# Graph network kernel: the row sums that give edges their places move from ScalarE to VectorE

## The reference

```python
# layer 0: sums of the edges' attributes by the edge's source
aggr_msg = jax.ops.segment_sum(edge_attr, row, num_segments=x.shape[0])   # row = src
h = jnp.concatenate([x, aggr_msg], axis=-1)                               # x normalised, relu
h = jax.nn.relu(h @ W1 + b1)
out = h @ W2 + b2
# layer 1: attention over the edges of a destination
z = h @ W_fc.T
a = z_src @ blk[0] + z_dst @ blk[K] + ex @ w_e      # and terms of moments
att = jnp.where(a > 0, a, SLOPE * a)
m = jax.ops.segment_max(att, dst, num_segments=N)
expv = jnp.exp(att - m[dst])
w = expv / denom[dst]
msg = w[:, None] * (z_src + ez)
return jax.ops.segment_sum(msg, dst, num_segments=N)
```

## Time and profile before

| | us |
|---|---|
| median of 3 runs | 5434.41 |
| lowest, highest | 5429.04, 5434.47 |
| profiled execution | 5417.05 |
| its span | 5415.2 |

### The profile page before, as it was taken

One profiled execution on the slowest core, in us unless ns is written; L12 is line 12 of the kernel. 1 busy time (PEld: TensorE's weight loads), 2 busy tenths in 40 slices (PEclk: granted clock), 3 DMA queues, 4 the chain that ended last, 5 costly groups with the idle time before them and its releaser, 6 DMA issues.

```text
span 5415.2 us, 60061 instructions
## 1 busy us (share of the span) xinstructions
PE 2284.4 (42%) x12501; PEld 1870.7 (35%) x12502; DVE 2997.1 (55%) x9197; ACT 2240.7 (41%) x9095; POOL 3005.6 (56%) x3151
## 2 busy tenths in 40 slices
PE   3545444545554555555786422222222222222222
PEld 1333333433444444444675322222222222222222
DVE  8555444445454555555664455555555555555556
ACT  2566666666555554543263222222222222222222
POOL 6556566555545555454503366666666666666662
PEclk9555555555555565555588655555555555555555
DMA  7433222322222232333331111222112221112212
GB/s 217 114 109 83 71 62 64 70 66 67 67 67 68 64 68 67 69 67 69 87 69 35 18 30 30 30 30 30 30 29 30 30 30 29 29 30 30 30 30 64
DMA packets 726919, 308.40 MB, mean 57 GB/s; under 512 B 661869, under 2 KB 662029, under 8 KB 726480
## 3 DMA queue, kind: packets, MB, share of 16 engines
q1 hardware_dynamic: 612608, 160.26, 14.9%
q0 software_dynamic: 100032, 105.80, 9.6%
q10 hardware_dynamic: 13968, 39.17, 2.1%
HBM read 206.21 MB, written 98.73 MB: 56 GB/s over the span
## 4 chain that ended last, share of the span: by engine, by line
issue 26%; another core or an unknown queue 25%; DVE 25%; ACT 12%; PE 10%; DVEq 2%; DMA 0%; SPq 0%; POOL 0%; ACTq 0%; POOLq 0%
PE half_banks L990 4%; DVE work L1368 4%; ACT z_sb L707 3%; ACT ohp L723 3%; ACT ohj L725 3%; DVE oh_all L1281 2%; DVE work L1784 2%; DVE work L1776 2%; ACT half_banks L842 2%; DVEq L1357 1%; DVE zg L1381 1%; PE half_banks L1158 1%; PE half_banks L1008 1%; DVE tab L1802 1%
## 5 line engine op out<-in xcount | busy, mean ns | idle before, releaser
L615 POOL DMA_INDIRECT sorted_dram<-ea_sb,idx x1563 | 1515.2, 969 | 1194.8 <-ACT ea_sb L715 704.1
L643 POOL DMA_INDIRECT zg<-z_dram,idx x1563 | 1482.8, 949 | 968.7 <-issue 906.2
L990 PE MATMUL half_banks<-z_sb,zg 128*128 128x65 f32 x4280 | 903.7, 385 | 834.7 <-DVE work L1368 616.7
L990 PEld LDWEIGHTS half_banks<-z_sb,zg 128*128 128x128 f32 x4280 | 872.5, 299 | 977.1 <-DVE zg L1381 759.3
L1368 DVE TENSOR_TENSOR work<-work,half_banks 128x65 f32 x2140 | 463.7, 217 | 1004.6 <-remote 806.9
L1169 PE MATMUL low_banks<-ident,f_top 128*80 128x128 f32 x196 | 85.5, 436 | 1465.7 <-DVE f_top L1787 1415.4
L723 ACT ACTIVATE ohp<-trow,zg 128x128 bf16<-128x128 f32 x1568 | 478.1, 386 | 378.9 <-remote 297.2
L707 ACT ACTIVATE z_sb<-z_sb 128x98 f32<-128x98 f32 x1560 | 420.8, 271 | 503.6 <-issue 262.9
L842 ACT ACTIVATE half_banks<-half_banks,f_s 128x80 f32<-128x80 f32 x1568 | 357.5, 316 | 616.8 <-issue 469.7
L1169 PEld LDWEIGHTS low_banks<-ident,f_top 128*80 128x80 f32 x196 | 28.0, 143 | 1503.7 <-DVE f_top L1787 1451.8
L725 ACT ACTIVATE ohj<-trow,zg 128x98 bf16<-128x98 f32 x1568 | 464.2, 364 | 149.9 <-issue 147.9
(11 more groups left out here) (304 smaller groups left out, 3577.5 us busy)
## 6 DMA issues: line engine op xcount, KB each, us to landing
z_sb<-sorted_dram SPq DMA_DIRECT2D x592, 132.0 KB
ea_sb<-in_edge_attr_dram SPq DMA_DIRECT2D x195, 256.0 KB
sorted_dram<-ea_sb,idx POOLq DMA_INDIRECT x1563
zg<-z_dram,idx POOLq DMA_INDIRECT x1563
sorted_dram<-big_b ACTq DMA_DIRECT2D x4, 3333.0 KB
sorted_dram<-big_b ACTq DMA_DIRECT2D x4, 3069.0 KB
f_t<-t_dram SPq DMA_DIRECT2D x196, 40.0 KB
sorted_dram<-big_b ACTq DMA_DIRECT2D x4, 1353.0 KB, 10.9
```

Of the source, the lines that this page charges most:

```text
L615: g_.indirect_dma_start(out=sorted_dram[BUF[c]][:, :], out_offset=bass.IndirectOffsetOnAxis(ap=idx[0:n, m % 4, g:g + 1], axis=0), in_=ea_s ...
L643: g_.indirect_dma_start(out=zg[0:n, s, g, 0:ZW + 1], out_offset=None, in_=z_dram[:, :], in_offset=bass.IndirectOffsetOnAxis(ap=idx[0:n, s, ...
L990: ins = t_.matmul(banks[4 + n % 2][:, u * AW:(u + 1) * AW], oh_step[:, n % 2, u, :], es_sb[:, n % 4, u, 0:AW], start=True, stop=True)
```

## The change

VectorE's `rank(m)` now makes the place numbers of every macro by itself: behind the next macro's comparison it waits for its own product, sums 128x784 to 128x8 in one instruction (`tensor_reduce`), waits for that, waits for the scatters of macro m - 4, and converts. `rank_out` is gone from ScalarE, and so is VectorE's wait for the row sums. Two waits on VectorE and one on SyncE at the end of the stage go by the conversion's semaphore (`s_idx`) now.

```diff
-            def rank_out(m):
-
-                if m == 0:
-                    return
-                act.wait_ge(s_prod, m + 1)
-                if m >= 4:
-                    act.wait_ge(s_sc[m % 4], 16 * G * (m // 4))
-                for g in range(G):
-                    at = prod[:, m % 2, g * NB:(g + 1) * NB]
-                    ins = a_.activation(at, at, ACT.Copy, accum_out=pos_f[:, m % 4, g:g + 1])
-                ins.then_inc(s_red, 1)
-                act.wait_ge(s_red, m + 1)
-                a_.activation(idx[:, m % 4, :], pos_f[:, m % 4, :], ACT.Copy).then_inc(s_idx, 1)
...
-                rank_out(m)
                 row_sources(m)
...
             def rank(m):
 
                 dve.wait_ge(s_rank, m + 1)
-                if m >= 2:
-                    dve.wait_ge(s_red, m - 1)
                 v_.tensor_tensor(prod[:, m % 2, :].rearrange("p (h c) -> p h c", h=2), ranks,
                                  ohs[:, m % 2, :].rearrange("p (h c) -> p h c", h=2), ALU.mult).then_inc(s_prod, 1)
-                if m == 0:
-                    dve.wait_ge(s_prod, 1)
-                    v_.tensor_reduce(pos_f[:, 0, :], prod[:, 0, :].rearrange("p (g j) -> p g j", g=G), X_AXIS, ALU.add
-                                     ).then_inc(s_red, 1)
-                    dve.wait_ge(s_red, 1)
-                    v_.tensor_copy(idx[:, 0, :], pos_f[:, 0, :]).then_inc(s_idx, 1)
                 if m + 1 < NM:
                     rank_onehots(m + 1)
+                dve.wait_ge(s_prod, m + 1)
+                v_.tensor_reduce(pos_f[:, m % 4, :], prod[:, m % 2, :].rearrange("p (g j) -> p g j", g=G), X_AXIS, ALU.add
+                                 ).then_inc(s_red, 1)
+                dve.wait_ge(s_red, m + 1)
+                if m >= 4:
+                    dve.wait_ge(s_sc[m % 4], 16 * G * (m // 4))
+                v_.tensor_copy(idx[:, m % 4, :], pos_f[:, m % 4, :]).then_inc(s_idx, 1)
...
-            dve.wait_ge(s_red, NM)
+            dve.wait_ge(s_idx, NM)
```

More of the change, by code:

```diff
@@ L504, in _ @@
             sp.wait_ge(s_sp, N0)
-            sp.wait_ge(s_red, NM)
+            sp.wait_ge(s_idx, NM)
             for i in range(GN[NCH - 1]):
```

## The result

The changed kernel took 5529.68 us (median of 4, 5526.62 to 5544.14), the kernel before 5431.73 us (5423.4 to 5434.47) beside it: a ratio of 1.0188, 95% interval 1.0167 to 1.021. It is slower, by 98 us; forecast were 5380 us and a gain. The profiled execution has a span of 5528.6 us against 5415.2.

A forecast was written before the change was run, and what follows sets the result against it. Bound: a chain between engines plus stalls, long after two macros' scatters in a row, short after one. Early +28, middle -104, first 8 and last 16 macros +26 us, sum -50: 5434 to 5380 us; range 5225 to 5600.

The forecast's parts named there:

- VectorE's cost: VectorE's added reduction and conversion: 1.08 us a macro, 195 x 1.08 = 211 us, all taken as path.
- The added wait for the scatter of four macros ago: VectorE, before the conversion: priced at 0, since place numbers are at most three macros ahead.
- ScalarE's relief: Row sums and conversion leave ScalarE: 2.4 to 2.9 us a macro, busy time down by more than 600 us.
- The early stages: 134 to 1328 us, 92 macros: 60% in pairs (two macros' scatters without a gap), 13.3 against 13.0 us, +28 us.
- The middle stages: 1328 to 2527 us, 80 macros: 85% singles (one macro's scatters per row), 13.7 against 15.0 us, -104 us.
- the rows of 16: Sign of being wrong: rows of 16 scatters, two macros without a gap, persist in 1328 to 2527 us.
- the 90 named: Sign in 1328 to 2527 us: VectorE's "remote" waits of 442.3 us must shrink by at least 90 us.
- The last stage: Last scatter stage: must be slower, near 14 us a macro; if not, the 1.08 us was hidden.
- C: Rival, slower: two-macro rows stay and VectorE's 1.08 us lands whole, 5645 us, or 5575 with a third won back; chance 0.27.
- E: Rival, slower: the stall is a price of each macro, tied to no grouping of scatters, 5645 us; chance 0.08.
- B: Rival, faster: two-macro rows of scatters vanish wholly, -201 us, 5235 us; chance 0.20.
- D: Rival, same: ScalarE's row sums were off the path and VectorE's gap takes the reduction, 5434 us; chance 0.10.

The follow-up runs named there:

- before_single_2: Kernel before, plus a GpSimd wait for the landing of the previous macro's scatters before each macro's scatters, on a stalling chip: 5316.07 us, 0.9698.
- before_single_half: Kernel before, GpSimd waiting for the previous macro's landing and again after the first four scatters within a macro, on a stalling chip: 5403.19 us, 0.9852.
- after_hold: Changed kernel, ScalarE waiting for a macro's place numbers and doing one 128x768 scratch activation before copying the source column: 5621.08 us, 1.0242.
- after_act_waits: Changed kernel, ScalarE waiting for VectorE's product before copying the source column and making its signs, without sums: 5606.97 us, 1.0218.
- after_sums_behind: Changed kernel, ScalarE's row sums put back into scratch, behind the source column's copy instead of ahead of it: 5591.4 us, 1.0189.
- before_plus_reduce: Kernel before, VectorE's reduction and conversion added into scratch, ScalarE's sums kept: 4300.4 us, 1.0138 on the calm chip; second run 5513.0 us, 1.005 on a stalling one.
- before_again: Kernel before, unchanged, run again on a stalling chip: 5488.51 us, 1.0015.

## Why the prediction was wrong

**VectorE's cost.** Forecast 1.08 us a macro, 211 us, all of it path. Busy time rose from 2997.1 to 3211.7 us, 214.6, the reduction takes 0.959 us and the conversion 0.172: the size is right. As path the whole change is 158 us without scatters, and this addition alone 30 us with the stalls. The added wait for the scatter of four macros ago was priced at nothing, and the conversion has no idle time ahead of it. The conversions took nothing from GpSimd that shows either: its scatters last 969 ns on average in both kernels.

**ScalarE's relief** was forecast as over 600 us of busy time. It is 2240.7 - 1720.5 = 520 us, since an activation and its accumulator reading overlap: 2.67 us a macro. Its worth is the first step that failed. I read GpSimd's 704.1 us of waiting for ScalarE as a loss that ends with the sums. Measured, the relief costs 90 us (5598 against 5508). My reading is that the wait was what let VectorE run ahead, and that its store of place numbers fed GpSimd in the stalls; that isn't shown. And line 715, priced at 0.1 us a macro because it stands ahead of its macro's signs, stands behind those of the macro before: 384.0 us of GpSimd's idle time still end there.

**The early stages.** Forecast 60% of macros in pairs, +28 us. Instead rows got longer: in 135 to 1413 us 10 rows of one macro, 18 of two, 9 of three and 4 of four, where the kernel before had 10 of one, 39 of two and one of three. The loss was 84 us. I had assumed that place numbers further apart break rows up. But by the count the long rows aren't what is dear. From the start of a row to that of the next, a macro took 16.6, 14.2, 13.3 and 12.8 us in rows of one, two, three and four, and in the kernel before 13.8 in rows of one and 12.8 in rows of two. The sum had a slip as well: the pairs got the 1.1 us, the singles at 12.1 didn't. With it the same shares give 0.6 x 14.2 + 0.4 x 13.2 = 13.8 us a macro, +74 us and not +28, and the forecast would have been no change.

**The middle stages.** Singles do outnumber pairs as forecast, 30 to 20, though the 20 pairs are also the rows of 16 whose persistence was named as a sign of being wrong; VectorE's unnamed waits at the group sums fell from 442.3 us to 317.5, by more than the 90 named. **The step that failed here, and with it the forecast gain of 104 us, is the prices: a single at 12.1 + 1.1 = 13.2 us, a pair at 15.5 + 1.1 = 16.6 us a macro.** 12.1 was one interval, of a stage whose mean is 194 / 15 = 12.9. In the middle stages of the same trace, counted over all rows, a macro took 16.4 us in the 19 singles and 14.6 in the 29 pairs. (With a limit of 0.4 us for the end of a row it is 15.9 and 14.6.) After the change it is 15.6 and 14.8. So a single was never the cheap state there, and more singles could not give 3.4 us a macro back: a single is a place where GpSimd found nothing ready after one macro and had to wait. VectorE's timeline of the changed kernel, in the last stage, from one product to the next shows what can be in such a macro:

```profile
2710.50 0.97 DVE L1282 TENSOR_TENSOR z_sb<-low_banks,oh_all 128x784 f32<-128x784 f32 x1
...
2716.64 0.22 DVE L1352 TENSOR_TENSOR work<-work,half_banks 128x65 f32 x1 [3.21 <-remote]
...
2723.72 0.22 DVE L1352 TENSOR_TENSOR work<-work,half_banks 128x65 f32 x1 [5.57 <-issue]
...
2731.17 0.97 DVE L1282 TENSOR_TENSOR z_sb<-low_banks,oh_all 128x784 f32<-128x784 f32 x1
```

This macro takes 20.67 us with two long waits in it, more than the stage's mean of 15.1. 20.67 - 3.21 - 5.57 = 11.9 us are work with its short waits, and GpSimd's next scatter comes at 2734.37, after an idle time of 10.87 us that ends with VectorE's conversion. As an estimate from this one macro, 11.9 us and one short stall of 3.26 us make 15.2: without a lead a macro costs VectorE's whole work and the stall, one behind the other. Instead of 104 us, 9 were gained.

**The last stage.** Forecast near 14 us a macro; it is 226 / 15 = 15.1, against 12.9. Here too the lead went, from 5 to 3 us, and twice the 1.08 us is lost.

**The rivals.** C (slower, pairs stay, 5575 to 5645) had the sign, and half its mechanism: the rows stayed and grew, but VectorE's 1.08 us is not what landed. E's price, the same for each macro, is refuted by before_single_2 and before_single_half, in which the same macros in shorter rows stall less or not at all; B by the rows; D by the loss. The Trainium skill's rule on page "SBUF — State Buffer", section "SBUF: two separate sides", that engine and DMA ports can't contend, agrees with the calm chip, where VectorE has no unnamed wait beside the scatters. It doesn't explain the 829.5 us of the stalling one, and I have no cause for these.

**What is shown and what is argued.** Shown: the scatters cause the stalls; a gap shortens them and rows of four end them; VectorE's half of the change costs 0.5% and the relief 1.6%; with the gap the change gains. Argued: that the lead is the link between relief and loss. It fits after_hold and after_act_waits, where the lead stayed short and the time high. after_sums_behind speaks against it as the whole story, since there the lead came back in part and the time didn't fall; no run set the lead alone. A rival is untested: the source column behind ScalarE's signs, for which GpSimd still waits 384.0 us, could be copied ahead of them. Open: what in a stalling chip holds VectorE and TensorE while GpSimd scatters, and why the second half, which has gathers and no scatters, is 476 us longer there too (2694 against 2218 us).

## What to carry over

Price a state (a single macro, a pair) by the mean over all its cases in the trace, and not by one interval: here that count alone would have taken the forecast gain away. Take it, too, only from a place where the engines stand to each other as they will after the change. A wait that looks like waste may be what keeps a store filled between two engines: before you remove it, measure how far the producer is ahead of the consumer. And where a large part of the idle time has no name in the trace, see the kernel on another chip before a change is built on it.

## What the runs showed of the hardware

The same program took 4241.66 us in one batch on one chip and 5480 us on another, 29% more; the busy times of before_plus_reduce on the one and of its second run on the other agree within 3% for each engine, and within 0.5% for the groups shown above. On the stalling chips GpSimd's indirect scatters at 1.26 us each go on while VectorE stands for up to 24 us (24.2 in after_hold, 16.3 in before_again) and TensorE with it. It needs a row of them: VectorE has no unnamed waits in rows of four (5 us) with landings between, 591.9 us of them in all at its group sums with rows of eight, 829.5 us with rows of eight to 24. A scatter's landing takes about 2.0 us after the last issue on both chips.
